# Attention block on one core: row maxima turned by one rounded product a query tile, diagonal tiles masked in PSUM by VectorE

## The chip, the cores and the metric

The kernel runs on one core of a Trainium2 chip. The metric is the device time of one execution in microseconds (us), lower is better.

## The reference

Two sequences of 2048 rows with 256 features pass through a layer norm, an attention of 16 heads with 64 features each, its output projection, a second norm, a small gated network and a third norm. What matters here is the attention:

```python
q = rope(hn @ Wq + bq); k = rope(hn @ Wk + bk); v = hn @ Wv + bv
attn = einsum('bihd,bjhd->bhij', q, k) * 64 ** -0.5
attn = where(tril, attn, -inf)
out = einsum('bhij,bjhd->bihd', softmax(attn), v) @ Wo + bo + h
```

Every softmax subtracts a row maximum before the exponential. Any number near the maximum does, as long as it is the same one for the whole row.

## The kernel before

**Pairs and groups.** Sixteen passes (`it` 0 to 15: eight pairs of heads for each of two sequences) run one behind the other. In a pass the two heads `a` of the pair lie on partitions 0 to 63 and 64 to 127. Queries are taken in four blocks of 512, keys in tiles of 128, so a pass has 40 score units (`UNITS`), two to a group, and 20 groups `g`. Every engine has its own list of work per group, written out by hand in `pair` of that engine, and the engines meet at counting semaphores.

**Work of PE (TensorE) in a group.** The order, in `pair` of the tensor block, is: first maxima unit, the group's two score units (L1221, L1223, L1225 and L1227, for diagonal units also the mask products L1231), second maxima unit, then in some groups the turning of the maxima (L1243, `turn_maxima`, in groups 1, 5, 11 and 19), or a piece of the next pass's projections (L1155 to L1157, groups 3, 4, 7, 8, 10, 13, 15, 17), a third maxima unit where there is one, the weighing of the values of the group before (L1261), and in groups 0, 2, 6 and 12 the sums of the exponentials (L1268).

**The maxima.** For the shift of the softmax the kernel computes the scores a second time, with the queries on partitions, coarsely. A maxima unit (t, c) is query tile t of 128 rows against key block c of up to 512 keys; `MUNITS` lists 40 of them a pass, and for each t the last one (c = t // 4) holds the diagonal. PE writes both heads' products into the single buffer `m_ps` (L1200). For a diagonal unit it then adds the causal mask on the last 128 keys by four small bf16 products (L1205: a mask of 64 rows times a 64 by 64 identity, two column halves for two heads). DVE (VectorE) takes the negated maximum over the keys from `m_ps` (L875) into `mpart`, and for the last unit of a tile reduces the parts into `mc` (L878). `mc` has one column for each block, tile and head. Maxima unit m + 1 may overwrite `m_ps` only when DVE has counted `maxed` for unit m; PE waits for that in `some_maxima`.

**The order on DVE in a group** (`pair` of the vector block): `turn_sums` (L915) of an ended block, `products` of the next pass's piece (L891, L895), the first two maxima, `piece_lo` (L909), `weights`, `invert` and `divide` (L920, L923, L928), `turned_sum` (L902, which waits for four DMAs that swap the halves of a head), and the third maximum.

**The turn.** The maxima must lie along the free axis of the score units. `turn_maxima` does this by eight fp32 products a block: for each of four tiles and each head, the column of `mc`, broadcast to 64 columns, is the stationary operand and the fp32 identity `id_f` the moving one; the result is 64 equal rows in each half of `x_ps`. ACT copies it, rounded to f32r, into `aux` (L599). In the scores, L1227 adds it by a product with `ones_r`, a matrix of 1/64, over the 64 equal rows of the head. An fp32 product shows as two MATMUL records in the trace, an f32r product as one.

```python
            def some_maxima(which):
                for m in which:
                    pe.wait_ge(maxed, it * NM + m)
                    maxima(it, par, m) ...
```

Of the kernel before, what the change touches and what calls it, by code (L numbers as in the profile page):

```python
# [5 lines left out]
ALU = mybir.AluOpType  # L6
ACT = mybir.ActivationFunctionType
AX = mybir.AxisListType
F32 = mybir.dt.float32
# [93 lines left out]
def postln_block_kernel(nc, h, gamma, beta, wqkv, bqk, bv, wo, bo, wgate_t, wup_t, wdown_t,  # L103
                        cos, sin, ident, masks, attn, hn_far, v_far, out):
    h, out = h.rearrange("b s d -> (b s) d"), out.rearrange("b s d -> (b s) d")
    with ExitStack() as ctx:
        def sb(name, shape, dt):
            return ctx.enter_context(nc.sbuf_tensor(name, shape, dt))
# [7 lines left out]
        cos_sb = sb("cos_sb", [P, SEQ], F32)  # L116
        sin_sb = sb("sin_sb", [P, SEQ], F32)
        id_f = sb("id_f", [P, P], F32)
        mask_b = sb("mask_b", [P, 4, P], BF16)
        id_b = sb("id_b", [P, DK], BF16)  # L120
        ones_r = sb("ones_r", [P, P], F32R)
        ones_f = sb("ones_f", [P, DK], F32)
        gam = sb("gam", [P, KC], F32)
        bet = sb("bet", [P, KC], F32)
# [1 line left out]
        w_raw = sb("w_raw", [P, KC, 2, P], F32)  # L126
        b_qk = sb("b_qk", [P, 2, 2], F32)
        b_v = sb("b_v", [P, OC], F32)
        mc = sb("mc", [P, BLOCKS, TG, 2], F32)
        mpart = sb("mpart", [P, 2, 2, BLOCKS], F32)  # L130
        r_i = sb("r_i", [P, NB // 32], F32)
        stats = sb("stats", [P, BATCH * TT, 6], F32)
# [128 lines left out]
        wv_hi = sem("wv_hi")  # L261
        wv_lo = sem("wv_lo")
        m_scored = sem("m_scored")
        maxed = sem("maxed")
        m_rows = sem("m_rows")
        m_turned = sem("m_turned")
        aux_done = sem("aux_done")
        scored = sem("scored")
# [64 lines left out]
        def _(sp):  # L333
# [124 lines left out]
            load_input(0, 3)  # L458
            load_b(0, 0)
            for dst, src in ((sin_sb[:, :], sin), (cos_sb[:, :], cos),  # L460
                             (mask_b[:, :, :], masks[:, 0:4 * P].rearrange("p (m n) -> p m n", m=4)),
                             (id_b[:, :], masks[:, 4 * P:4 * P + DK]), (b_v[:, :], bv),
                             (bo_sb[:, :], bo.partition_broadcast(P))):
                sp.dma_start(dst, src).then_inc(const_in, 16)
            for g in range(GROUPS):
# [109 lines left out]
        def _(act):  # L575
# [156 lines left out]
            affine(2)  # L732
            affine(3)
            root_input(3)
            for t in range(TG):
                evict_v_first(t)
            for i in range(4, TURNS):
# [83 lines left out]
        @block.vector  # L821
        def _(dve):
            nc.vector.memset(ones_f[:, :], 1.0).then_inc(o_stored, 16)
            nc.vector.memset(ones_r[:, :].bitcast(F32), 1.0 / DK).then_inc(out_stored, 16)
            nc.vector.memset(mc[:, :, :, :], 0.0).then_inc(normed, 1)
            nc.vector.memset(r_i[:, :], 0.0).then_inc(tile_done, 1)
            nc.vector.memset(pause[:, :], 0.0).then_inc(z_added, 1)
            nc.vector.memset(rstd[:, :], 0.0).then_inc(primed, 1)
# [35 lines left out]
            def weights(n):  # L864
                dve.wait_ge(w_hi, n + 1)
                nc.vector.tensor_tensor(w_hl[:, 1, :, :], w_raw[:, :, :, :].rearrange("p k j n -> p k (j n)"),
                                        w_hl[:, 0, :, :].bitcast(F32), ALU.subtract).then_inc(w_lo, 1)

            def maximum(n, m):

                t, c, w = MUNITS[m]
                dve.wait_ge(m_scored, n * NM + (m + 1))
                parts = t // TG + 1
                dst = mc[:, t // TG, t % TG, :] if parts == 1 else mpart[:, t % 2, :, c]
                nc.vector.tensor_reduce(dst, m_ps[:, :, 0:w], AX.X, ALU.max, negate=True).then_inc(maxed, 1)  # L875
                if parts > 1 and c == parts - 1:
                    dve.wait_ge(maxed, n * NM + (m + 1))
                    nc.vector.tensor_reduce(mc[:, t // TG, t % TG, :], mpart[:, t % 2, :, 0:parts],  # L878
                                            AX.X, ALU.min).then_inc(m_rows, 1)

            def rest_wv(n, raw):
# [271 lines left out]
        def _(pe):  # L1153
# [38 lines left out]
            def maxima(n, par, m):  # L1192

                t, c, w = MUNITS[m]
                if c == 0 and t % TG == 0:
                    pe.wait_ge(qk_hi, n * (2 * BLOCKS) + 2 * (t // TG + 1))
                diag = c == t // TG
                q, k = slice(t * P, (t + 1) * P), slice(NB * c, NB * c + w)
                for a, rows in enumerate(halves):
                    last = nc.tensor.matmul(m_ps[:, a, 0:w], qk[par][rows, 0, q], qk[par][rows, 1, k],  # L1200
                                            start=True, stop=not diag)
                if diag:
                    for x in range(2):
                        for a, rows in enumerate(halves):
                            last = nc.tensor.matmul(m_ps[:, a, w - P + DK * x:w - P + DK * (x + 1)],  # L1205
                                                    mask_b[rows, 2 + x, :], id_b[rows, :], start=False, stop=x == 1)
                last.then_inc(m_scored, 1)

            def scores(kind, it, par, u):
                blk, j, q0 = UNITS[u]  # L1210
                if kind is not FIRST or u >= 2:
                    pe.wait_ge(exped, it * NU + (u - 1))
                if j == 0:
                    pe.wait_ge(aux_done, it * BLOCKS + (blk + 1))
                    pe.wait_ge(qk_lo, it * (2 * BLOCKS) + 2 * (blk + 1))
                q, k = slice(NB * blk + q0, NB * (blk + 1)), slice(j * P, (j + 1) * P)
                two = 2 * (u % 2)
                dst = [s_ps[:, two + a, q0:NB] for a in range(2)]
                diag = j >= 4 * blk
                for a, rows in enumerate(halves):  # L1220
                    nc.tensor.matmul(dst[a], qk[par][rows, 1, k], qk[par][rows, 0, q], start=True, stop=False)  # L1221
                for a, rows in enumerate(halves):
                    nc.tensor.matmul(dst[a], qk[par][rows, 1, k], qk[par][rows, 2, q], start=False, stop=False)  # L1223
                for a, rows in enumerate(halves):
                    nc.tensor.matmul(dst[a], qk[par][rows, 3, k], qk[par][rows, 0, q], start=False, stop=False)  # L1225
                for a, rows in enumerate(halves):
                    last = nc.tensor.matmul(dst[a], ones_r[rows, :], aux[rows, q0:NB], start=False, stop=not diag)  # L1227
                if diag:
                    for x in range(2):
                        for a, rows in enumerate(halves):  # L1230
                            last = nc.tensor.matmul(s_ps[:, two + a, q0 + DK * x:q0 + DK * (x + 1)],  # L1231
                                                    mask_b[rows, x, :], id_b[rows, :], start=False, stop=x == 1)
                last.then_inc(scored, 1)

            def turn_maxima(n, blk):

                if blk == 0:
                    pe.wait_ge(maxed, n * NM + TG)
                else:
                    pe.wait_ge(m_rows, n * (TT - TG) + TG * blk)  # L1240
                for t in range(TG):
                    for a, rows in enumerate(halves):
                        last = nc.tensor.matmul(x_ps[rows, t * P:(t + 1) * P], mc[:, blk, t, a:a + 1].broadcast_to([P, DK]),  # L1243
                                                id_f[:, :], start=True, stop=True, skip_group_check=True)
                last.then_inc(m_turned, 1)

            def weigh(kind, it, par, g):
# [143 lines left out]
            for m in range(TG, 2 * TG):  # L1391
                first_maximum(m)
                project_v_first(2 * TG + m)
            pe.wait_ge(v_done, TT - 1)
            turn_maxima(0, 0)
            for m in range(2 * TG, PROLOGUE_MAXIMA):
                first_maximum(m)
# [140 lines left out]
```

## Time and profile before

| what | value |
|---|---|
| time, median of 3 runs | 2189.78 us (2185.9 to 2190.99) |
| the profiled execution: its time | 2190.48 us |
| its span in the trace | 2188.7 us |
| PE busy | 2073.8 us, 95% |
| DVE busy | 1549.2 us, 71% |
| ACT / POOL busy | 915.9 us / 1401.2 us |
| mean granted TensorE clock | 0.986 of full speed |

Busy time counts the union of the intervals of an engine's instructions. PE's matmuls are pipelined and overlap in the records, so a record's length (0.40 us for 512 columns) is not what the matmul takes from the stream: that is the distance from one start to the next. "PEld" is the loading of the stationary operand, which can run beside an earlier matmul.

### The profile page before, as it was taken

Reading aid. Unit: us, or ns where it says so; the run is one execution under the profiler, and the core shown is the slowest. Engines: PE = TensorE matmul, PEld = TensorE weight load, DVE = VectorE, ACT = ScalarE, POOL = GpSimd, SP = SyncE. Lnnn points to the kernel's source line nnn. Section 1 sums busy time; section 2 is a strip of 40 time slices with the busy share of each in tenths; the row PEclk is TensorE's granted clock in tenths of the full one; section 3 lists DMA queues with packets and bytes.
Section 4 is the critical chain, followed back from the end, with each engine's and each line's share of the span. In section 5 each row is a group of like instructions: output and inputs, shape, how many; then the busy total and the mean of one; then the engine's idle time right before and its main releaser. Section 6 shows DMA issues by size and latency. Waiting matters only on the chain.

```text
span 2188.7 us, 38909 instructions
## 1 busy us (share of the span) xinstructions
PE 2073.8 (95%) x15488; PEld 1311.4 (60%) x15488; DVE 1549.2 (71%) x2181; ACT 915.9 (42%) x1262; POOL 1401.2 (64%) x1206
## 2 busy tenths in 40 slices
PE   6889999999999999999999999999999989999997
PEld 5555555555555555555555555555555545788986
DVE  7577767676778776767767777767777765666654
ACT  4434343444343434434344444443444344534442
POOL 3368777777787876677878787878787878100000
PEclk9899999999999999999999999999999999999999
DMA  6411212121212122122121212121112131222200
GB/s 207 132 44 46 57 42 61 38 65 35 61 32 63 33 74 69 46 67 68 44 59 44 59 44 59 44 59 34 49 35 55 34 131 44 76 93 75 98 10 29
DMA packets 116154, 132.25 MB, mean 60 GB/s; under 512 B 15248, under 2 KB 71184, under 8 KB 115728
## 3 DMA queue, kind: packets, MB, share of 16 engines
q1 hardware_dynamic: 115984, 129.92, 20.1%
q8 instruction: 115, 1.88, 0.4%
q14 instruction: 55, 0.45, 0.1%
HBM read 56.47 MB, written 39.85 MB: 44 GB/s over the span
## 4 chain that ended last, share of the span: by engine, by line
PE 68%; DVE 20%; DMA 3%; issue 3%; SPq 3%; ACT 2%; POOL 1%; ACTq 0%; DVEq 0%
PE o_ps L1261 15%; DVE mpart L875 8%; PE m_ps L1200 8%; PE s_ps L1221 5%; PE s_ps L1225 4%; PE s_ps L1227 4%; PE s_ps L1223 4%; PE x_ps L1155 3%; DMA rot<-qr 3%; SPq L387 3%; DVE qc L902 3%; PE x_ps L1243 3%; PE x_ps L1268 2%; PE x_ps L1157 2%; PE x_ps L1156 2%
## 5 line engine op out<-in xcount | busy, mean ns | idle before, releaser
L561 POOL TENSOR_TENSOR acc<-acc,pt 128x512 f32<-128x512 f32 (+3 forms) x1024 | 1199.1, 1204 | 209.5 <-ACT pt L615 209.1
L875 DVE TENSOR_REDUCE mpart<-m_ps 128x2 f32<-128x1024 f32 (+2 forms) x576 | 625.0, 1085 | 309.6 <-PE m_ps L1200 227.4
L615 ACT ACTIVATE pt<-s_ps 128x1024 f32<-128x1024 f32 (+3 forms) x640 | 544.3, 896 | 701.4 <-PE s_ps L1227 334.3
L1261 PE MATMUL o_ps<-pt,v 128*64 128x512 f32 (+3 forms) x2560 | 538.1, 541 | 0.0
L1200 PE MATMUL m_ps<-qk 64*128 64x512 f32 (+3 forms) x1280 | 288.1, 446 | 62.6 <-DVE mpart L875 52.9
L1200 PEld LDWEIGHTS m_ps<-qk 64*128 64x128 f32 x1280 | 120.7, 185 | 367.9 <-DVE mpart L875 211.4
L1261 PEld LDWEIGHTS o_ps<-pt,v 128*64 128x64 f32 x2560 | 159.7, 137 | 222.6 <-issue 202.6
L556 POOL TENSOR_TENSOR acc<-pt 128x512 f32<-128x512 f32 (+1 forms) x128 | 166.8, 1325 | 160.5 <-ACT pt L615 160.5
L1221 PE MATMUL s_ps<-qk 64*128 64x512 f32 (+3 forms) x1280 | 253.4, 392 | 0.0
L1225 PE MATMUL s_ps<-qk 64*128 64x512 f32 (+3 forms) x1280 | 234.7, 362 | 0.0
L1227 PE MATMUL s_ps<-aux,ones_r 64*128 64x512 f32 (+3 forms) x1280 | 234.7, 362 | 0.0
L1223 PE MATMUL s_ps<-qk 64*128 64x512 f32 (+3 forms) x1280 | 234.1, 362 | 0.0
L902 DVE TENSOR_TENSOR qc<-qc,rot 128x512 f32<-128x512 f32 x128 | 141.2, 1105 | 101.7 <-DMA rot<-qr 101.5
L593 ACT ACTIVATE qk<-qc 128x512 fp32r<-128x512 f32 x128 | 80.2, 629 | 221.0 <-DVE qc L902 221.0
L909 DVE TENSOR_TENSOR qk<-qc,qk 128x512 fp32r<-128x512 f32 x120 | 139.0, 1158 | 0.0
L1225 PEld LDWEIGHTS s_ps<-qk 64*128 64x128 f32 x1280 | 121.2, 185 | 19.7
L1227 PEld LDWEIGHTS s_ps<-aux,ones_r 64*128 64x128 f32 x1280 | 121.2, 185 | 19.0
L1223 PEld LDWEIGHTS s_ps<-qk 64*128 64x128 f32 x1280 | 121.9, 186 | 17.2
L1221 PEld LDWEIGHTS s_ps<-qk 64*128 64x128 f32 x1280 | 121.9, 187 | 15.6 <-ACT pt L615 4.1
L1155 PE MATMUL x_ps<-hn,w_hl 128*128 128x512 f32 x240 | 108.4, 452 | 0.0
L1156 PE MATMUL x_ps<-hn,w_hl 128*128 128x512 f32 x240 | 95.4, 397 | 0.0
L1157 PE MATMUL x_ps<-hn,w_hl 128*128 128x512 f32 x240 | 95.2, 397 | 0.0
(168 smaller groups left out, 2883.1 us busy)
## 6 DMA issues: line engine op xcount, KB each, us to landing
rot<-qr SPq DMA_DIRECT2D x512, 64.0 KB, 2.0
attn<-o_sum SPq DMA_DIRECT2D x64, 256.0 KB, 2.3
o_raw<-attn SPq DMA_DIRECT2D x8, 2048.0 KB, 9.0
v<-v_far SPq DMA_DIRECT2D x16, 768.0 KB, 5.3
v_far<-v_part SPq DMA_DIRECT2D x48, 256.0 KB, 2.0
w_raw<-in_wqkv SPq DMA_DIRECT2D x34, 128.0 KB, 4.8
v_far<-v SPq DMA_DIRECT2D x16, 256.0 KB, 2.6
v<-v_far SPq DMA_DIRECT2D x16, 256.0 KB, 4.5
```

What stands on the lines that cost most here:

```text
L556: last = nc.gpsimd.tensor_tensor(sums, pt[:, (u - 1) % SLOTS, a, q0:NB], probs, ALU.add)
L561: nc.gpsimd.tensor_tensor(sums, sums, probs, ALU.add).then_inc(summed, 1)
L615: nc.scalar.activation(pt[:, u % SLOTS, :, q0:NB], s_ps[:, two:two + 2, q0:NB], ACT.Exp, scale=SCALE)\
L875: nc.vector.tensor_reduce(dst, m_ps[:, :, 0:w], AX.X, ALU.max, negate=True).then_inc(maxed, 1)
L902: nc.vector.tensor_tensor(qc[:, c % 2, a, :], qc[:, c % 2, a, :], rot[:, a, :], ALU.add).then_inc(roped, 1)
L1155: nc.tensor.matmul(dst, lhs[0], rhs[0], start=first, stop=False)
L1200: last = nc.tensor.matmul(m_ps[:, a, 0:w], qk[par][rows, 0, q], qk[par][rows, 1, k], start=True, stop=not diag)
L1221: nc.tensor.matmul(dst[a], qk[par][rows, 1, k], qk[par][rows, 0, q], start=True, stop=False)
L1223: nc.tensor.matmul(dst[a], qk[par][rows, 1, k], qk[par][rows, 2, q], start=False, stop=False)
L1225: nc.tensor.matmul(dst[a], qk[par][rows, 3, k], qk[par][rows, 0, q], start=False, stop=False)
L1227: last = nc.tensor.matmul(dst[a], ones_r[rows, :], aux[rows, q0:NB], start=False, stop=not diag)
L1261: last = nc.tensor.matmul(o_ps[rows, q0:NB], v[par][:, j, rows], pt[:, u % SLOTS, a, q0:NB], start=(j == 0), stop=(j == n - 1), skip_group ...
```

## The change

It has two edits and what they need.

1. The turn: `mc` becomes f32r, DVE rounds when it writes the maxima, and has 132 columns a block. The maxima of tile t of a block go to columns t (head 0) and 64 + t (head 1). The slice of 128 columns that begins at t is the stationary operand of one f32r product with a rounded identity `id_r`; row 0 of the result holds the maxima of head 0, row 64 those of head 1, other rows hold values that nobody uses. `ones_r` becomes `pick_r`, zero but for ones in rows 0 and 64, so that L1227's product, of unchanged size, picks the row. There are four products a block in place of eight.
2. The mask of the maxima: PE's four mask products a diagonal unit go. DVE adds a bf16 mask of 128 by 128 to the last 128 keys of both heads in `m_ps`, waits until the result has landed, and then takes the maximum.

The mask products of the score units (L1231) stay.

```diff
-        mask_b = sb("mask_b", [P, 4, P], BF16)
+        id_r = sb("id_r", [P, P], F32R)
+        mask_b = sb("mask_b", [P, 3, P], BF16)
-        ones_r = sb("ones_r", [P, P], F32R)
+        pick_r = sb("pick_r", [P, P], F32R)
-        mc = sb("mc", [P, BLOCKS, TG, 2], F32)
+        mc = sb("mc", [P, BLOCKS, P + TG], F32R)
...
             root_input(3)
+            nc.scalar.activation(id_r[:, :], id_f[:, :], ACT.Copy).then_inc(id_rounded, 1)
...
-            nc.vector.memset(ones_r[:, :].bitcast(F32), 1.0 / DK).then_inc(out_stored, 16)
-            nc.vector.memset(mc[:, :, :, :], 0.0).then_inc(normed, 1)
+            nc.vector.memset(pick_r[:, :].bitcast(F32), 0.0).then_inc(out_stored, 15)
+            dve.wait_ge(out_stored, 15)
+            for a in range(2):
+                last = nc.vector.memset(pick_r[DK * a:DK * a + 1, :].bitcast(F32), 1.0)
+            last.then_inc(out_stored, 1)
+            nc.vector.memset(mc[:, :, :].bitcast(F32), 0.0).then_inc(normed, 1)
...
+            def row_maxima(t):
+                return mc[:, t // TG, 0:P].rearrange("p (a i) -> p a i", a=2)[:, :, t % TG]
+
             def maximum(n, m):
 
                 t, c, w = MUNITS[m]
                 dve.wait_ge(m_scored, n * NM + (m + 1))
                 parts = t // TG + 1
-                dst = mc[:, t // TG, t % TG, :] if parts == 1 else mpart[:, t % 2, :, c]
+                dst = row_maxima(t) if parts == 1 else mpart[:, t % 2, :, c]
+                if c == parts - 1:
+
+                    own = m_ps[:, :, w - P:w]
+                    nc.vector.tensor_tensor(own, own, mask_b[:, 2, :].unsqueeze(1).broadcast_to([P, 2, P]),
+                                            ALU.add).then_inc(m_masked, 1)
+                    dve.wait_ge(m_masked, n * TT + (t + 1))
                 nc.vector.tensor_reduce(dst, m_ps[:, :, 0:w], AX.X, ALU.max, negate=True).then_inc(maxed, 1)
                 if parts > 1 and c == parts - 1:
                     dve.wait_ge(maxed, n * NM + (m + 1))
-                    nc.vector.tensor_reduce(mc[:, t // TG, t % TG, :], mpart[:, t % 2, :, 0:parts],
+                    nc.vector.tensor_reduce(row_maxima(t), mpart[:, t % 2, :, 0:parts],
                                             AX.X, ALU.min).then_inc(m_rows, 1)
...
-                diag = c == t // TG
...
                     last = nc.tensor.matmul(m_ps[:, a, 0:w], qk[par][rows, 0, q], qk[par][rows, 1, k],
-                                            start=True, stop=not diag)
-                if diag:
-                    for x in range(2):
-                        for a, rows in enumerate(halves):
-                            last = nc.tensor.matmul(m_ps[:, a, w - P + DK * x:w - P + DK * (x + 1)],
-                                                    mask_b[rows, 2 + x, :], id_b[rows, :], start=False, stop=x == 1)
+                                            start=True, stop=True)
...
-                    last = nc.tensor.matmul(dst[a], ones_r[rows, :], aux[rows, q0:NB], start=False, stop=not diag)
+                    last = nc.tensor.matmul(dst[a], pick_r[rows, :], aux[rows, q0:NB], start=False, stop=not diag)
...
                 for t in range(TG):
-                    for a, rows in enumerate(halves):
-                        last = nc.tensor.matmul(x_ps[rows, t * P:(t + 1) * P], mc[:, blk, t, a:a + 1].broadcast_to([P, DK]),
-                                                id_f[:, :], start=True, stop=True, skip_group_check=True)
+                    last = nc.tensor.matmul(x_ps[:, t * P:(t + 1) * P], mc[:, blk, t:t + P],
+                                            id_r[:, :], start=True, stop=True, skip_group_check=True)
...
             pe.wait_ge(v_done, TT - 1)
+            pe.wait_ge(id_rounded, 1)
             turn_maxima(0, 0)
```

## Rows read from the trace of the kernel before

**Rows 1.** The page: busy time and share of the span, then the chain by engine.
```profile
PE 2073.8 (95%) x15488; PEld 1311.4 (60%) x15488; DVE 1549.2 (71%) x2181; ACT 915.9 (42%) x1262; POOL 1401.2 (64%) x1206
PE 68%; DVE 20%; DMA 3%; issue 3%; SPq 3%; ACT 2%; POOL 1%; ACTq 0%; DVEq 0%
```

**Rows 2.** Timeline of PE in pass 8: start us, length us, then the instruction.
```profile
1006.70 0.27 PE L1227 MATMUL s_ps<-aux,ones_r 64*128 64x128 f32 x2
1006.81 0.23 PE L1231 MATMUL s_ps<-id_b,mask_b 64*128 64x64 bf16 x4
1006.98 1.09 PE L1243 MATMUL x_ps<-id_f,mc 128*64 128x128 f32 x16
1007.90 1.67 PE L1261 MATMUL o_ps<-pt,v 128*64 128x512 f32 x8
...
1053.84 0.39 PE L1156 MATMUL x_ps<-wv_hl,hn 128*128 128x512 f32 x1
1054.07 0.39 PE L1157 MATMUL x_ps<-wv_hl,hn 128*128 128x512 f32 x1
1054.39 1.94 PE L1261 MATMUL o_ps<-pt,v 128*64 128x512 f32 x8
```

**Rows 3.** Groups of instructions, 1868 to 1871 us: busy us, mean ns, idle before.
```profile
L1410 PE MATMUL gu_ps<-id_f,x_g 128*128 128x128 f32 x8 | 1.1, 280 | 2.1 <-DVE x_g L1043 2.1
```

**Rows 4.** Waits, whole span: us in total, times, longest us.
```profile
PEld o_ps L1261 <- ACT pt L615: 7.8, 30, 0.3
DVE qc L902 <- DMA rot<-qr: 101.5, 78, 3.9
```

**Rows 5.** Timeline of PE, diagonal unit (11, 2), then the next maxima unit.
```profile
1124.63 0.50 PE L1200 MATMUL m_ps<-qk 64*128 64x512 f32 x2
1124.97 0.24 PE L1205 MATMUL m_ps<-id_b,mask_b 64*128 64x64 bf16 x4
1125.04 0.48 PE L1221 MATMUL s_ps<-qk 64*128 64x512 f32 x2
1125.35 0.40 PE L1223 MATMUL s_ps<-qk 64*128 64x512 f32 x2
1125.58 0.40 PE L1225 MATMUL s_ps<-qk 64*128 64x512 f32 x2
...
1126.97 0.40 PE L1200 MATMUL m_ps<-qk 64*128 64x512 f32 x2
```

**Rows 6.** Groups of instructions on DVE by shape, whole span.
```profile
L891 DVE SCALAR_TENSOR_TENSOR qr<-x_ps,b_qk,sin_sb 128x512 f32<-128x512 f32 x120 | 88.8, 740 | 2.3 <-PE x_ps L1157 2.3
L1113 DVE SCALAR_TENSOR_TENSOR out_g<-z_ps,x_keep 128x512 f32<-128x512 f32 x2 | 1.4, 688 | 4.3 <-PE z_ps L1157 4.3
L875 DVE TENSOR_REDUCE mpart<-m_ps 128x2 f32<-128x512 f32 x48 | 32.6, 679 | 31.5 <-PE m_ps L1205 31.5
L875 DVE TENSOR_REDUCE mpart<-m_ps 128x2 f32<-128x256 f32 x48 | 20.3, 422 | 20.1 <-PE m_ps L1205 20.1
L883 DVE TENSOR_TENSOR wv_hl<-wv_raw,wv_hl 128x512 fp32r<-128x512 f32 x6 | 8.1, 1347 | 1.5 <-ACT wv_hl L624 1.5
```

**Rows 7.** Timeline of DVE in pass 9: units (11, 2), (4, 1), (5, 0) and (13, 3).
```profile
1125.39 1.19 DVE L875 TENSOR_REDUCE mpart<-m_ps 128x2 f32<-128x1024 f32 x1
1126.61 0.16 DVE L878 TENSOR_REDUCE mc<-mpart 128x2 f32<-128x6 f32 x1
...
1076.52 0.41 DVE L875 TENSOR_REDUCE mpart<-m_ps 128x2 f32<-128x256 f32 x1
...
1078.35 1.22 DVE L875 TENSOR_REDUCE mpart<-m_ps 128x2 f32<-128x1024 f32 x1
...
1147.97 0.65 DVE L875 TENSOR_REDUCE mpart<-m_ps 128x2 f32<-128x512 f32 x1
```

**Rows 8.** Timeline of PE in pass 9: the maxima units behind (5, 0) and (13, 3).
```profile
1079.62 0.39 PE L1200 MATMUL m_ps<-qk 64*128 64x256 f32 x2
...
1148.67 0.50 PE L1200 MATMUL m_ps<-qk 64*128 64x512 f32 x2
```

More of the change, by code:

```diff
@@ L263, in postln_block_kernel @@
         m_scored = sem("m_scored")
+        m_masked = sem("m_masked")
         maxed = sem("maxed")
         m_rows = sem("m_rows")
+        id_rounded = sem("id_rounded")
         m_turned = sem("m_turned")
@@ L460, in _ @@
             for dst, src in ((sin_sb[:, :], sin), (cos_sb[:, :], cos),
-                             (mask_b[:, :, :], masks[:, 0:4 * P].rearrange("p (m n) -> p m n", m=4)),
-                             (id_b[:, :], masks[:, 4 * P:4 * P + DK]), (b_v[:, :], bv),
+                             (mask_b[:, :, :], masks[:, 0:3 * P].rearrange("p (m n) -> p m n", m=3)),
+                             (id_b[:, :], masks[:, 3 * P:3 * P + DK]), (b_v[:, :], bv),
                              (bo_sb[:, :], bo.partition_broadcast(P))):
@@ L1508 @@
     r, k = np.arange(P)[:, None] % DK, np.arange(P)[None, :]
-    masks = [np.where(later, np.float32(MASKED), np.float32(0))
-             for later in (k > r, k > r + DK, r > k, r + DK > k)]
+    row = np.arange(P)[:, None]
+    masks = [np.where(later, np.float32(MASKED), np.float32(0)) for later in (k > r, k > r + DK, k > row)]
     def with_first(a, n):
```

## The prediction

> **What bounds the kernel now.** I read the page first, then PE's timeline over two groups of a pass, then DVE's timeline beside it. The page shows PE busy for 95% and DVE for 71%, and a chain that is PE for 68% and DVE for 20% [rows 1]. So a microsecond off PE's stream is worth something in most places, but in a fifth of the span DVE is what everything waits for, and the change takes from PE and gives to DVE. The question is at which of the sixteen diagonal units of a pass PE has time to spare and at which it waits for `maxed`. That is read unit by unit from the two timelines, as the distance between the end of DVE's reduction and the next L1200.
>
> Three patterns are seen. In the first the next L1200 comes 0.5 to 0.6 us behind the end of the reduction (tiles 1, 2 and 6) or over 2 us behind (tiles 0, 5, 8, 9, 10, 12 and 15), as a weighing of up to 1.9 us lies between [rows 2]. In the second DVE ends little before: unit (11, 2) ends at 1125.39 + 1.19 = 1126.58 and the next L1200 starts at 1126.97 [rows 5, 7]. In the third PE is held: the reduction of (13, 3) ends at 1147.97 + 0.65 = 1148.62, and L1200 starts at 1148.67 [rows 7, 8].
>
> **Edit 1, the turn.** The sixteen records of L1243 take from 1006.98 to 1007.90, 0.92 us of PE's stream [rows 2], once in each of 64 blocks. The new turn is four products of 128 columns with a full array of weights. Nothing of that form is in the attention, but the eight transposes of the same form L1410 take 1.1 us in all with a last record of 0.28, so (1.1 - 0.28) / 7 = 0.12 us each [rows 3], and a pair of score products of 128 columns takes 1006.81 - 1006.70 = 0.11 [rows 2]. I take 0.11. The last one is followed by a weighing in another tiling of the array; at such a change, from L1157 to L1261, 0.32 us pass where 0.23 pass between like products (1053.84 to 1054.07) [rows 2]. A 512-column stream accounts for 0.23 - 0.02 = 0.21, so 0.11 are the change of tiling, and behind a stream of a quarter the length, 0.05, the step is 0.16 us. The new turn: 3 x 0.11 + 0.16 = 0.49 us, a saving of 0.43. What comes in front (1006.81 to 1006.98) stays. Bounds: 3 x 0.05 + 0.16 = 0.31 us if only the stream counted (saving 0.61), and 4 x 0.28 = 1.12 us if nothing overlapped (a loss of 0.20); I stay at the transposes and the score pairs, the nearest rows.
>
> Is it paid? The turn is always followed by the weighing, which hardly waits for ACT (7.8 us in 30 waits over the whole span) [rows 4], so the stream moves up at once. In groups 1, 11 and 19 the maxima units behind it have over 2 us in hand. In group 5 they do not: DVE is then in a sequence of `products`, swap by DMA and `turned_sum` (101.5 us of DVE's waits are for that DMA [rows 4]) that began before the turn, and the unit after the next is held by it. There I count nothing. So three turns a pass: 48 x 0.43 = **21 us off**.
>
> Against this stands a rule of the Trainium skill, page "TensorE: Matmul & The Clock Gate", section on packing small matmuls: a weight load runs beside an earlier matmul only if the two use different row groups, which the new full-array products do not. By it each product would pay its load and its stream, by the page's formula for loads an estimated 107 + 53 = 160 ns, and edit 1 would save some 10 us less. The transposes at 0.12 us use the same row groups and speak against it.
>
> **Edit 2 on PE.** At unit (11, 2) the four mask products hold the stream from 1124.97 to 1125.04, 0.07 us, and the first score product behind them takes 0.31 (1125.04 to 1125.35) where the next takes 0.23, so 0.08 more: together 0.15 us [rows 5]. I take 0.15 us for every diagonal unit, sixteen a pass. It is paid where PE is not held afterwards: nine of the first pattern, 9 x 16 x 0.15 = **22 us off**. For tile 12 (unit (12, 3)), I count nothing, as with the turn of group 5 that follows it.
>
> **Edit 2 on DVE.** The added add reads two heads of 128 columns from PSUM with a bf16 operand from SBUF and writes PSUM. Nothing in the trace writes PSUM from DVE. The nearest rows are operations on PSUM with an SBUF operand: 740 ns and 688 ns for 512 columns [rows 6]. The reduction shows the slope, 679 ns for 512 and 422 for 256, so 257 ns less for half: 0.43 to 0.48 us; I take 0.44, as the mask is small and L891 runs evenly beside POOL's work. The reduction must wait until the result has landed. DVE's dependent step L878 starts 1126.61 - 1126.58 = 0.03 us after its source ended [rows 7]. So a maximum becomes **0.47 us** later, and 256 of them add 120 us to DVE's busy 1549. Bounds: 0.26 us if only the columns counted (the slope alone), and 0.74 + 0.03 if a write to PSUM doubled the work.
>
> Who waits for it: the reduction stands behind the add, everything later in DVE's list behind both, and PE's next maxima unit behind the count.
> - Pattern 1: hidden. Where the gap is near 0.55 (tiles 1, 2, and the unit (6, 1)), 0.55 - 0.05 covers 0.47 barely.
> - Pattern 2: L1200 starts 0.39 after DVE ended; a held one starts 0.05 after, but with 0.11 of weight load inside its record (0.50 against 0.40 long [rows 5, 8]). The cover is 0.39 - 0.05 - 0.11 = 0.23, the delay 0.47 - 0.23 = 0.24. There are three a pass, tiles 3, 7 and 11: 0.72 us.
> - Pattern 3: the whole 0.47, at tiles 13 and 14; and at tile 4, because its reduction at 1076.52, L891, L895 and the next reduction, that ends at 1078.35 + 1.22 = 1079.57, stand without a gap, and PE starts at 1079.62 [rows 7, 8]. Three a pass: 1.41 us.
> - Tile 12's add lies in DVE's wait for the swap of halves, and costs nothing; if that wait were gone it would cost another 0.47.
>
> Sum: 2.13 us x 16 = **34 us on**. In some passes DVE is further behind than in the two that I read unit by unit, where it splits weights (L883, six times, 1347 ns [rows 6]) or the next sequence's input (eight times): some ten stretches in which a saving is lost and an add paid, about 0.5 us each, **5 us on**.
>
> **The rest.** ACT's rounding of the identity, two short memsets and a larger one of `mc` lie ahead of the first loads' landing or beside PE's prologue; the mask DMA is smaller. L1227 keeps its shape. Each at nothing; if the cover were gone, under 1 us in all. The eight diagonal units of the prologue are inside the sixteen passes counted.
>
> **Sum.** 21 + 22 - 34 - 5 = 4 us off. Against the profiled execution's own 2190.5 us that is 2186.5; that execution lay 0.7 above the median of the three, so **2186 us**.
>
> **The rivals.**
> 1. *DVE becomes the bound (slower).* Place: the adds at tiles 13, 14, 4, and 3, 7, 11. Each 0.1 us more for the add costs 6 x 16 x 0.1 = 9.6 us, so from 0.51 us for add and wait on nothing is gained, and from 0.56 the kernel is slower by over 0.2%. With the upper bound 0.77 the six cost 29 us more and the three of 0.5 cover begin to delay PE by 0.3 each, 14 more: 2229. For it: no row of DVE writing PSUM, and the order on DVE, where L902 behind it also runs beside POOL. Against: 740 ns hardly vary. Chance 0.28.
> 2. *The adds hide better than I count.* If the delays of pattern 2 are taken up by the groups behind and the fourth turn is paid, 12 + 7 less: 2167. For it: DVE idles for 29% of the span. Chance 0.14.
> 3. *The new products do not overlap their weight loads*, and a turn takes 4 x 0.05 us more: 48 x 0.2 = 10 us, 2196. This is the rule cited above. Chance 0.05.
> 4. *The turn does not do what it says*, because ACT's copy or a wait behind it holds the stream anyway: 21 us back, 2207. Against it stands the 7.8 us of waits. Chance 0.05.
>
> **How the numbers follow.** My forecast has 0.48, with its own range of 2178 to 2195. About 0.2%, 4.4 us, is what a measurement of this kernel can tell from no change. The forecast lies on that edge: of its 0.48 I give 0.26 to faster, 0.17 to no change, 0.05 to slower. Rival 1 gives 0.24 to slower and 0.04 to no change, rival 2 all to faster, rival 3 half to either, rival 4 all to slower. Faster 0.40, same 0.24, slower 0.36. The range takes in most of rival 2 and rival 1 up to an add of 0.65: 2168 to 2208.
>
> **What would show it.** Right: L1243's four products within 0.5 us of the stream; no L1205; the first score product behind a diagonal unit at 0.23; the add at 0.42 to 0.48 us; DVE busy near 1665 us; idle of L1200 behind DVE up, at tiles 3, 4, 7, 11, 13 and 14 alone. Wrong: an add over 0.55 us, L1200 held behind tiles 1, 2 or 6, `turned_sum` or `products` late behind the adds with PE waiting for `x_ps`, or turns of 0.7 us.

## The result, and the profile of the changed kernel

The changed kernel takes 2240.45 us (median of 4 runs, 2237.5 to 2246.3) against 2190.39: a ratio of 1.0234, 95% interval 1.0222 to 1.0247. It is 50 us slower, outside the range that was given, and on the side of rival 1. The ground that rival 1 was priced by did not come, though: the add takes what was forecast.

The page of the changed kernel, busy times and chain by engine, which answer to [rows 1], then the costliest maxima group of PE:

```profile
PE 2064.5 (92%) x13696; PEld 1271.7 (57%) x13696; DVE 1674.2 (75%) x2439; ACT 918.0 (41%) x1263; POOL 1405.8 (63%) x1206
PE 50%; DVE 33%; DMA 5%; issue 5%; SPq 5%; ACT 2%; POOL 1%; ACTq 0%; DVEq 0%
L1216 PE MATMUL m_ps<-qk 64*128 64x512 f32 (+3 forms) x1280 | 296.5, 460 | 127.6 <-DVE mpart L892 94.5
```

PE lost 9 us of busy time and 1792 records, as it should. DVE gained 125 us, near the 120 forecast. The chain went from 68% PE and 20% DVE to 50% and 33%, and DMA with its issue (SPq), which is mostly the swap of halves, from 6% to 10%: PE sets the pace in half of the span where it did in two thirds.

Groups of DVE, busy us, mean ns, idle before. In the kernel before:

```profile
L902 DVE TENSOR_TENSOR qc<-qc,rot 128x512 f32<-128x512 f32 x128 | 141.2, 1105 | 101.7 <-DMA rot<-qr 101.5
L909 DVE TENSOR_TENSOR qk<-qc,qk 128x512 fp32r<-128x512 f32 x120 | 139.0, 1158 | 0.0
L928 DVE TENSOR_TENSOR o_sum<-o_sum,r_t 128x512 f32<-128x512 f32 x64 | 56.7, 887 | 2.2
```

and in the changed one:

```profile
L919 DVE TENSOR_TENSOR qc<-qc,rot 128x512 f32<-128x512 f32 x128 | 136.3, 1067 | 82.0 <-DMA rot<-qr 81.9
L889 DVE TENSOR_TENSOR m_ps<-m_ps,mask_b 128x256 f32<-128x256 f32 x256 | 107.8, 421 | 91.3 <-PE m_ps L1216 91.0
L926 DVE TENSOR_TENSOR qk<-qc,qk 128x512 fp32r<-128x512 f32 x120 | 146.6, 1222 | 0.0
L945 DVE TENSOR_TENSOR o_sum<-o_sum,r_t 128x512 f32<-128x512 f32 x64 | 68.9, 1076 | 2.2
```

The add (L889) takes 421 ns; 0.44 us was assumed. The nearest operation that reads PSUM and SBUF and writes SBUF, L1084 in the same trace, takes 684 ns for 512 columns; less the 257 ns of the slope that is an estimated 427 ns for 256, so no extra price of writing PSUM is to be seen. What was not forecast are the other rows, three operations with both operands in SBUF and the same work as before. `piece_lo` (L909 before, L926 now) and the division (L928, L945) have become longer, 139.0 to 146.6 us and 56.7 to 68.9 us; `turned_sum` (L902, L919) has become shorter, 141.2 to 136.3 us.

**Where the time went.** The distances between the starts of consecutive maxima units on PE, averaged over passes 1 to 15 of both traces, add up to a pass. The largest differences, in us a pass (a minus is faster):

| from unit to unit | before | changed | difference |
|---|---|---|---|
| (0, 0) to (1, 0), holds a turn | 4.25 | 3.88 | -0.37 |
| (9, 2) to (10, 0), holds a turn | 4.09 | 3.66 | -0.43 |
| (10, 2) to (11, 0), holds a turn | 4.15 | 3.72 | -0.43 |
| (13, 0) to (13, 1), holds a turn | 4.39 | 4.03 | -0.35 |
| (1, 0) to (2, 0) | 2.24 | 2.60 | +0.36 |
| (3, 0) to (4, 0) | 2.34 | 3.51 | +1.17 |
| (7, 0) to (7, 1) to (8, 0) | 4.81 | 5.83 | +1.03 |
| (12, 1) to (12, 2) | 3.03 | 3.81 | +0.78 |
| (13, 3) to (14, 0) | 2.38 | 2.83 | +0.45 |
| all forty | | | +3.3 |

3.3 us in sixteen passes are 53 us: the whole loss. It sits in a handful of places, and the turn is a gain wherever PE runs freely.

The largest place, tile 3, on DVE's timeline. Before:

```profile
1066.59 0.69 DVE L902 TENSOR_TENSOR qc<-qc,rot 128x512 f32<-128x512 f32 x1 [2.86 <-DMA rot<-qr]
1067.20 0.68 DVE L875 TENSOR_REDUCE mc<-m_ps 128x2 f32<-128x512 f32 x1
1069.17 0.96 DVE L875 TENSOR_REDUCE mc<-m_ps 128x2 f32<-128x768 f32 x1 [1.28 <-PE m_ps L1205]
1070.04 0.68 DVE L909 TENSOR_TENSOR qk<-qc,qk 128x512 fp32r<-128x512 f32 x1
1070.83 0.72 DVE L915 STREAM_TRANSPOSE r_t<-x_ps 128x512 f32<-128x512 f32 x1
1071.47 1.19 DVE L875 TENSOR_REDUCE mc<-m_ps 128x2 f32<-128x1024 f32 x1
```

Changed:

```profile
1096.36 0.69 DVE L919 TENSOR_TENSOR qc<-qc,rot 128x512 f32<-128x512 f32 x1 [3.50 <-DMA rot<-qr]
1096.97 0.43 DVE L889 TENSOR_TENSOR m_ps<-m_ps,mask_b 128x256 f32<-128x256 f32 x1
1097.43 0.69 DVE L892 TENSOR_REDUCE mc<-m_ps 128x2 fp32r<-128x512 f32 x1
1098.66 0.43 DVE L889 TENSOR_TENSOR m_ps<-m_ps,mask_b 128x256 f32<-128x256 f32 x1 [0.54 <-PE m_ps L1216]
1099.13 0.96 DVE L892 TENSOR_REDUCE mc<-m_ps 128x2 fp32r<-128x768 f32 x1
1100.01 1.45 DVE L926 TENSOR_TENSOR qk<-qc,qk 128x512 fp32r<-128x512 f32 x1
1101.37 0.70 DVE L932 STREAM_TRANSPOSE r_t<-x_ps 128x512 f32<-128x512 f32 x1
1102.00 0.40 DVE L889 TENSOR_TENSOR m_ps<-m_ps,mask_b 128x256 f32<-128x256 f32 x1
1102.43 1.23 DVE L892 TENSOR_REDUCE mc<-m_ps 128x2 fp32r<-128x1024 f32 x1
```

Two things are to be seen. First, the stretch begins with `turned_sum` at the landing of a DMA. PE's unit (1, 0) had long been there (1094.73), so what PE saved ahead of it became a longer wait: from (0, 0) to (2, 0) the changed kernel is 0.01 us a pass faster than the one before, where the kernel without any mask of the maxima (`turn_no_mask`, below) is 0.43 faster. Second, L926 takes 1.45 us where it took 0.68. POOL's timeline over the same place, changed kernel:

```profile
1099.62 2.99 POOL L559 TENSOR_TENSOR acc<-pt 128x512 f32<-128x512 f32 x2 [4.59 <-ACT pt L618]
```

and before:

```profile
1070.10 3.03 POOL L556 TENSOR_TENSOR acc<-pt 128x512 f32<-128x512 f32 x2 [3.58 <-ACT pt L615]
```

Before, DVE's instruction began 0.06 us ahead of POOL's two additions and ran at its own speed; it was POOL's first addition that took 1.77 us, and its second 1.30. Now DVE's begins at 1100.01, 0.39 us behind POOL's start. By the two records behind POOL's merged row its first addition takes 1.28 and ends at 1100.90, and its second takes 1.75; DVE's instruction ends 0.55 us behind that first addition, at 1101.45. By the Trainium skill, page "SBUF — State Buffer", section "SBUF: two separate sides", an instruction of DVE with two SBUF inputs and one of GpSimd that reads SBUF exclude each other, and whoever starts first keeps the shared ports to its end. These rows agree: each waits for the other's end. The adds, with one operand in PSUM, take 0.39 to 0.43 us in all 256 places and never grow, which agrees too. The prediction did not use the rule.

### The profile page after: what moved, and what is told of

Its sections match the earlier page's. It is cut to its first block, busy times and chain, and to the rows that moved or that the text cites. A ratio compares the mean times of both kernels' runs of the same rounds, so it can differ in the third digit from the quotient of the medians.

```text
span 2244.5 us, 35584 instructions
## 1 busy us (share of the span) xinstructions
PE 2064.5 (92%) x13696; PEld 1271.7 (57%) x13696; DVE 1674.2 (75%) x2439; ACT 918.0 (41%) x1263; POOL 1405.8 (63%) x1206
## 4 chain that ended last, share of the span: by engine, by line
PE 50%; DVE 33%; DMA 5%; issue 5%; SPq 5%; ACT 2%; POOL 1%; ACTq 0%; DVEq 0%
DVE mpart L892 11%; PE o_ps L1271 11%; PE m_ps L1216 7%; DMA rot<-qr 5%; SPq L390 5%; DVE qk L926 4%; DVE qc L919 3%; DVE qr L908 3%; PE s_ps L1232 3%; PE s_ps L1236 2%; PE s_ps L1238 2%; PE s_ps L1234 2%; DVE m_ps L889 2%; PE x_ps L1172 2%; PE gu_ps L1172 2%
## 5 line engine op out<-in xcount | busy, mean ns | idle before, releaser
L1271 PE MATMUL o_ps<-pt,v 128*64 128x512 f32 (+3 forms) x2560 | 544.7, 547 | 0.0
L1216 PE MATMUL m_ps<-qk 64*128 64x512 f32 (+3 forms) x1280 | 296.5, 460 | 127.6 <-DVE mpart L892 94.5
L1271 PEld LDWEIGHTS o_ps<-pt,v 128*64 128x64 f32 x2560 | 156.9, 137 | 234.2 <-issue 201.6
L1238 PE MATMUL s_ps<-aux,pick_r 64*128 64x512 f32 (+3 forms) x1280 | 237.4, 366 | 0.0
L919 DVE TENSOR_TENSOR qc<-qc,rot 128x512 f32<-128x512 f32 x128 | 136.3, 1067 | 82.0 <-DMA rot<-qr 81.9
L889 DVE TENSOR_TENSOR m_ps<-m_ps,mask_b 128x256 f32<-128x256 f32 x256 | 107.8, 421 | 91.3 <-PE m_ps L1216 91.0
L926 DVE TENSOR_TENSOR qk<-qc,qk 128x512 fp32r<-128x512 f32 x120 | 146.6, 1222 | 0.0
L1238 PEld LDWEIGHTS s_ps<-aux,pick_r 64*128 64x128 f32 x1280 | 122.3, 187 | 19.6
L1172 PE MATMUL x_ps<-hn,w_hl 128*128 128x512 f32 x240 | 108.2, 451 | 0.0
L1173 PE MATMUL x_ps<-hn,w_hl 128*128 128x512 f32 x240 | 95.4, 397 | 0.0
```

Of the source, the lines that this page charges most:

```text
L919: nc.vector.tensor_tensor(qc[:, c % 2, a, :], qc[:, c % 2, a, :], rot[:, a, :], ALU.add).then_inc(roped, 1)
L926: nc.vector.tensor_tensor(qk[par][:, 2 + a, here], qc[:, c % 2, a, :], qk[par][:, a, here].bitcast(F32), ALU.subtract).then_inc(qk_lo, 1)
L1172: nc.tensor.matmul(dst, lhs[0], rhs[0], start=first, stop=False)
L1238: last = nc.tensor.matmul(dst[a], pick_r[rows, :], aux[rows, q0:NB], start=False, stop=not diag)
L1271: last = nc.tensor.matmul(o_ps[rows, q0:NB], v[par][:, j, rows], pt[:, u % SLOTS, a, q0:NB], start=(j == 0), stop=(j == n - 1), skip_group ...
```

## The experiments

### One edit at a time, and PE's side without DVE's

`turn_alone` has edit 1 with the masks of the maxima left to PE:

```diff
+DVE_MASKED = ()
...
-                if c == parts - 1:
+                if c == parts - 1 and t in DVE_MASKED:
 
                     own = m_ps[:, :, w - P:w]
...
+                on_pe = c == t // TG and (True)
+                if on_pe:
+                    for x in range(2):
+                        for a, rows in enumerate(halves):
+                            last = nc.tensor.matmul(m_ps[:, a, w - P + DK * x:w - P + DK * (x + 1)],
+                                                    mask_b[rows, 3 + x, :], id_b[rows, :], start=False, stop=x == 1)
```

> Edit 1 alone; the masks of the maxima stay on PE. Theory A (in the changed kernel the adds stand one behind another in DVE's list, in stretches that no PE event starts, and nearly all of them are paid; the turn itself is a gain): the turn takes 0.5 us less of PE's stream in each of 64 blocks or a little less, part of it swallowed by waits for maxed, so 12 to 22 us below the kernel before. Theory B (the new turn or what hangs on it is at fault: full-array products, the copy, the picking product): at or above the kernel before, up to +50 us.

Measured: 2182.75 us, ratio 0.9953 (0.9936 to 0.9970). Edit 1 is a gain of 7 us by the medians (the interval allows 7 to 14), so Theory B falls; the gain is at the lower end of what Theory A gave or under it.

`mask_alone` is the kernel before with edit 2 alone (`turn_maxima`, `mc` and `ones_r` as before; L1205 out, DVE's add in).

> Edit 2 alone: the turn is the one of before by fp32 products, DVE adds the mask. Theory A: the whole loss and more, 60 to 75 us above the kernel before. Theory B: under 20 us above it.

Measured: 2246.36 us, ratio 1.0255 (1.0223 to 1.0286), 56 us above. The whole loss is edit 2's. It is a little under the range of Theory A and far from Theory B.

`turn_no_mask` takes the add out and puts nothing in, so its maxima run over later keys of the diagonal tile too:

```diff
+DVE_MASKED = ()
...
-                if c == parts - 1:
+                if c == parts - 1 and t in DVE_MASKED:
```

> The changed kernel without any mask of the maxima: neither PE's products nor DVE's add, so the row maxima are taken over later keys of the diagonal tile too (the scores of the softmax keep their mask). It shows what PE's side of both edits is worth without DVE's. Theory A: 30 to 45 us below the kernel before, 80 to 95 us below the changed one. Theory C (DVE was the bound all along and PE's savings are worth little): under 20 us below the kernel before, by the turn alone or less.

Measured: 2155.13 us, ratio 0.9826 (0.9792 to 0.9860), 28 us below `turn_alone` and 85 below the changed kernel. PE's half of edit 2 is worth 28 us, if DVE gets nothing in return. Both figures lie in Theory A's ranges, and Theory C falls.

`turn_both_masks` puts PE's products back and keeps the add (of the diff of `turn_alone`, the part from `on_pe` on alone).

> The changed kernel with PE's mask products put back beside DVE's add, so the mask is added twice. Against turn_alone it is the price of 256 adds and their waits on DVE and nothing else. Theory A: 5 to 15 us above the changed kernel and 70 to 85 us above turn_alone, that is 0.3 us for each add of 0.45. Theory C (the removal of the mask products was worth nothing): the same time as the changed kernel.

Measured: 2234.59 us, ratio 1.0193 (1.0162 to 1.0224). The 256 adds cost 2234.59 - 2182.75 = 52 us, 0.20 us each, under the 70 to 85 of Theory A. The surprise is the other comparison: with PE's 1024 mask products put back the kernel is 6 us faster than the changed one, not 5 to 15 slower. What saved 28 us without the adds saves nothing beside them, as Theory C had it. One place shows why that can be. DVE's timeline around the division ahead of unit (12, 1), changed kernel:

```profile
1160.36 0.71 DVE L940 STREAM_TRANSPOSE r_t<-r_i 128x512 f32<-128x512 f32 x1
1161.11 1.78 DVE L945 TENSOR_TENSOR o_sum<-o_sum,r_t 128x512 f32<-128x512 f32 x1
1162.81 1.21 DVE L892 TENSOR_REDUCE mpart<-m_ps 128x2 f32<-128x1024 f32 x1
```

and `turn_both_masks`:

```profile
1155.91 0.71 DVE L940 STREAM_TRANSPOSE r_t<-r_i 128x512 f32<-128x512 f32 x1
1156.66 0.71 DVE L945 TENSOR_TENSOR o_sum<-o_sum,r_t 128x512 f32<-128x512 f32 x1
1157.29 1.21 DVE L892 TENSOR_REDUCE mpart<-m_ps 128x2 f32<-128x1024 f32 x1
```

The same division takes 1.78 us in one and 0.71 in the other; in the mean over passes 1.72 and 0.71 (0.94 in the kernel before), and the step from (12, 1) to (12, 2) is 1.01 us a pass longer, 16 us in all. A saving of some tenths on PE moved the division into POOL's work. That accounts for 16 of the 34 us between a gain of 28 and a loss of 6; for the rest no single place was found.

### How much of the adds' price is POOL?

Both kernels have POOL's sums of the exponentials cut from up to 512 columns to 16, with a memset of `acc` ahead of the passes. They leave out most of the softmax's denominators:

```diff
-                        sums = acc[:, blk % 2, a, q0:NB]
-                        probs = pt[:, u % SLOTS, a, q0:NB]
+                        sums = acc[:, blk % 2, a, q0:q0 + 16]
+                        probs = pt[:, u % SLOTS, a, q0:q0 + 16]
```

> turn_alone with POOL's sums of the exponentials cut to 16 columns (the denominators are left out but for those), so that POOL hardly works beside DVE. DVE's instructions with two operands in SBUF (L902, L909, L928 of the kernel before) are to fall from 0.9 to 1.1 us in the mean to 0.7. Either theory: 15 to 50 us below turn_alone. It is the base for light_both_masks.

Measured: 2120.01 us, ratio 0.9677 (0.9658 to 0.9695), 63 us below `turn_alone` and more than expected. At most that much of the kernel's time hangs on DVE instructions that stand behind POOL's; whatever else waits for POOL gets shorter in this kernel too.

> turn_both_masks with POOL's sums cut to 16 columns (the denominators are left out but for those). Against light_turn_alone it is the price of the 256 adds without POOL beside DVE. Theory A1 (a shifted DVE falls into POOL's work, and that is a good part of the 52 us that the adds cost with POOL): 15 to 35 us above light_turn_alone. Theory A2 (the adds cost by their own length in series with PE's waits, POOL has no part): 45 to 60 us above it.

Measured: 2150.92 us, ratio 0.9823 (0.9805 to 0.9841). The adds now cost 2150.92 - 2120.01 = 31 us, against 52 with POOL at work. Groups of DVE in `light_both_masks`:

```profile
L922 DVE TENSOR_TENSOR qc<-qc,rot 128x512 f32<-128x512 f32 x128 | 89.1, 698 | 82.0 <-DMA rot<-qr 81.6
L929 DVE TENSOR_TENSOR qk<-qc,qk 128x512 fp32r<-128x512 f32 x120 | 82.4, 687 | 0.0
L948 DVE TENSOR_TENSOR o_sum<-o_sum,r_t 128x512 f32<-128x512 f32 x64 | 44.3, 692 | 2.2
```

All three stand at 0.69 to 0.70 us now. And at tile 3, on its timeline:

```profile
1044.67 0.68 DVE L929 TENSOR_TENSOR qk<-qc,qk 128x512 fp32r<-128x512 f32 x1
1045.27 0.71 DVE L935 STREAM_TRANSPOSE r_t<-x_ps 128x512 f32<-128x512 f32 x1
1045.90 0.40 DVE L892 TENSOR_TENSOR m_ps<-m_ps,mask_b 128x256 f32<-128x256 f32 x1
1046.34 1.23 DVE L895 TENSOR_REDUCE mc<-m_ps 128x2 fp32r<-128x1024 f32 x1
```

The measured 31 us lie in Theory A1's range and far from A2's: some 21 of the 52 us go with POOL's load. But they are not all instructions that the adds pushed behind POOL. Busy time of the three groups in each kernel, in us:

| | `turned_sum` | `piece_lo` | division | sum |
|---|---|---|---|---|
| `turn_alone` | 142.2 | 139.4 | 56.7 | 338.3 |
| `turn_both_masks` | 137.7 | 145.1 | 58.4 | 341.2 |
| `light_turn_alone` | 89.3 | 82.6 | 44.3 | 216.2 |
| `light_both_masks` | 89.1 | 82.4 | 44.3 | 215.8 |

With POOL at work the adds lengthen the three groups by 3 us in all: some instances grow and others shrink. What counts is where. At tile 3 `piece_lo` grows from 0.68 to 1.40 us, and the adds lengthen the step from (3, 0) to (4, 0) by 1.12 us a pass with POOL at work (`turn_both_masks` against `turn_alone`) and by 0.40 without. These 0.72 us are 12 of the 21 us. Other places point at a second reason: the step behind (13, 3) costs 0.43 us a pass with POOL and nothing without, and in the kernel without POOL's load DVE's list is 122 us shorter, so that DVE has time to spare there (in `turn_alone` PE starts 0.06 us behind the reduction of (13, 3), in `light_turn_alone` 0.71). This pair cuts POOL everywhere, so it does not part new collisions from the slack that the old ones had used up.

### Which adds are paid?

`adds_1_2_3` and `hybrid5` leave the mask to PE except for the named tiles (`t in DVE_MASKED` on DVE, `t not in DVE_MASKED` on PE).

> Edit 1, and DVE's add in place of PE's mask products for query tiles 1, 2 and 3 alone. The prediction counted 0.24 us a pass for them (tile 3) less 0.3 saved on PE, so about the time of turn_alone. Theory A (the three adds stand in one stretch of DVE's list that begins with turned_sum, so at the landing of a DMA and not at an event of PE; all are paid, and the piece_lo behind them falls into POOL's work and takes twice as long): 1.0 to 1.4 us a pass, 16 to 22 us above turn_alone, a third of the whole price for three of sixteen adds.

Measured: 2197.21 us, ratio 1.0032 (1.0021 to 1.0043), 14.5 us above `turn_alone`, a little under Theory A's range: 0.30 us for each of 48 adds, PE's savings already taken off. The places in its trace and in that of `turn_alone`, us behind unit (0, 0) on PE, means over passes 1 to 15:

| | `turn_alone` | `adds_1_2_3` |
|---|---|---|
| PE starts (2, 0) | 6.31 | 6.26 |
| PE starts (3, 0) | 8.34 | 8.28 |
| DVE starts `piece_lo` behind tile 2 | 7.67 | 8.07 |
| POOL starts its two additions | 7.85 | 7.71 |
| length of that `piece_lo` | 0.68 | 1.46 |
| PE starts (4, 0) | 10.69 | 11.80 |

The adds of tiles 1 and 2 are hidden from PE's units (2, 0) and (3, 0). But tile 2's leaves DVE's list behind it 0.40 us later, which puts `piece_lo` behind POOL's start instead of ahead of it, where it takes 0.78 us more; with the add of tile 3 all of it stands in front of the reduction that unit (4, 0) waits for.

> Edit 1, and DVE's add in place of PE's mask products for query tiles 5, 8, 9, 12 and 15 alone, the ones behind which the changed kernel shows PE's next maxima unit still 0.4 us or more behind DVE. Theory A (the price is set by the place of an add, not by its number): these five are hidden and PE's savings of 0.08 to 0.15 us each are kept, 3 to 9 us below turn_alone. Rival (each add costs 0.2 us wherever it stands, as DVE's share of the span is what counts): 5 x 16 x 0.2 less 8 = 8 us above it.

Measured: 2171.29 us, ratio 0.9911 (0.9889 to 0.9934), 11.5 us below `turn_alone`, a little more than Theory A gave, and 19 below the kernel before. Five adds a pass in the right places cost nothing that can be seen, and PE keeps 0.08 us at four of them and 0.15 at (9, 2), 7.5 us in all. The rest may be chance of timing: `piece_lo` takes 129.1 us in sum here and 139.4 in `turn_alone`. The rival of an equal price falls.

`hybrid5_twice` makes each of these five adds twice, with a wait each.

> hybrid5 with the add of its five tiles made twice, each time with its wait, so 80 adds of 0.45 us more in DVE's list and nothing else changed. Theory A (these places have 0.4 us and more behind the first add): 0 to 6 us above hybrid5, under 0.08 us an add. Rival (0.2 us an add wherever it stands): 16 us above it.

Measured: 2174.40 us (2164.3 to 2180.2), ratio 0.9930 (0.9903 to 0.9957). It lies 3 us above `hybrid5` and within its own spread. By the medians 80 adds more cost 0.04 us each there; at the average of 0.20 us it would have been 16, which is above the slowest of the four runs.

`hybrid7` hands tiles 0 and 10 to DVE as well.

> hybrid5 with tiles 0 and 10 handed to DVE as well. Tile 0's add lies in DVE's wait for the swapped halves, tile 10's ends ahead of PE's next but one. Theory A: PE saves 0.10 and 0.15 us a pass, the adds cost 0 to 0.15: from 4 us below hybrid5 to 2 above it. Rival (0.2 us for every add): 3 us above it and more.

Measured: 2171.12 us, ratio 0.9906 (0.9880 to 0.9932), the same as `hybrid5`. At tile 0 PE gains 0.10 us a pass and loses 0.06 of it at the next unit.

### A move that failed

`late_lo` puts `piece_lo` behind the group's other work in the changed kernel:

```diff
-                    if g - 2 in PIECE and kind is not LAST:
-                        piece_lo(it + 1, *PIECE[g - 2], 1 - par)
...
                     for m in ms[2:]:
                         maximum(it, m) if m < NM else maximum(it + 1, m - NM)
+                    if g - 2 in PIECE and kind is not LAST:
+                        piece_lo(it + 1, *PIECE[g - 2], 1 - par)
```

> The changed kernel with one step of DVE moved within its group: piece_lo, with both operands in SBUF, stands behind the third maximum and the division instead of ahead of them. The work is the same. Theory A1 (behind the adds piece_lo falls into POOL's work just where PE's next maximum waits for what is behind it, tile 3 above all): 8 to 20 us below the changed kernel, and the step from unit (3, 0) to (4, 0) shorter by 0.7 us or more. Theory A2 (the length of the adds alone): within 5 us of the changed kernel.

Measured: 2252.63 us, ratio 1.0275 (1.0248 to 1.0303), 12 us slower than the changed kernel. Neither theory's range holds it. It was ill chosen for the place it was meant for: group 12 has no third maximum and no `products`, so `piece_lo` still stands ahead of tile 3, whose step did not change (+0.03 us). Elsewhere the move did harm, above all behind (7, 1), +0.75 us a pass. It says nothing against or for the collision at tile 3.

> The same move in hybrid5, whose tiles 1 to 3 are masked by PE. Theory A1: little to gain, as piece_lo behind tile 2 takes 0.68 us there already: between 10 us below hybrid5 and 3 above it. A gain as large as that of late_lo over the changed kernel would say that the move is worth something whether the adds are there or not.

Measured: 2191.12 us, ratio 0.9995 (0.9981 to 1.0009), 20 us slower than `hybrid5`, outside the expectation. The move costs with and without the adds, and not by collisions: the three groups with two SBUF operands take 312 us in sum here and 325 in `hybrid5`, and 336 in `late_lo` against 352 in the changed kernel. What it costs by is the order. Behind (7, 0) in `hybrid5_late_lo`:

```profile
973.17 1.23 DVE L893 TENSOR_REDUCE mpart<-m_ps 128x2 f32<-128x1024 f32 x1 [0.87 <-PE m_ps L1218]
974.31 1.03 DVE L927 TENSOR_TENSOR qk<-qc,qk 128x512 fp32r<-128x512 f32 x1
975.26 0.74 DVE L909 SCALAR_TENSOR_TENSOR qr<-x_ps,b_qk,sin_sb 128x512 f32<-128x512 f32 x1
975.92 0.73 DVE L913 SCALAR_TENSOR_TENSOR qc<-x_ps,b_qk,cos_sb 128x512 f32<-128x512 f32 x1
976.58 1.21 DVE L893 TENSOR_REDUCE mpart<-m_ps 128x2 f32<-128x1024 f32 x1
```

`piece_lo` (L927) now stands between two reductions that PE waits for, with the products behind it; in `hybrid5` it stood ahead of the first, at 964.38, and ran while DVE had to wait for PE. The second reduction came 2.46 us behind the first there and comes 3.41 behind it here.

## Why the prediction was wrong

**The turn** was mis-sized. The four products and the way out of them, changed kernel, timeline of PE:

```profile
1092.32 0.23 PE L1242 MATMUL s_ps<-id_b,mask_b 64*128 64x64 bf16 x4
1092.48 0.66 PE L1253 MATMUL x_ps<-id_r,mc 128*128 128x128 f32 x4
1093.08 1.72 PE L1271 MATMUL o_ps<-pt,v 128*64 128x512 f32 x8
1094.73 0.39 PE L1216 MATMUL m_ps<-qk 64*128 64x256 f32 x2
```

They hold the stream for 1093.08 - 1092.48 = 0.60 us, where 0.49 was forecast and 0.92 stood before [rows 2]. The distances of their starts in the trace are 0.17, 0.11 and 0.11, and 0.20 to the weighing: the step of 0.11 between like products was right, and the first and the last cost 0.05 more each than forecast. The weighing behind takes 0.05 more as well, and in `turn_alone` the three free turns of a pass save 0.27 to 0.28 each, not 0.43: 13 us. The fourth, of group 5, for which nothing was counted, shortens its step by 0.41, of which the next loses 0.10. Other steps, above all the one behind (14, 3) with 0.24, become longer, and 7 us are left by the medians. By the rule of the Trainium skill that the prediction cites (page "TensorE: Matmul & The Clock Gate", section on packing small matmuls: full-array loads do not overlap a matmul) each product would take an estimated 0.16. The trace does not agree: the four weight loads start 0.11 us apart. That the sum comes near 4 x 0.16 = 0.64 is by the first and the last step.

**PE's mask products** were worth 0.15 us only behind (1, 0), (9, 2) and (10, 2); behind the other unhindered tiles, in `turn_no_mask` against `turn_alone`, 0.07 to 0.11. The 22 us were too many for the nine tiles; without the adds all sixteen give 28.

**The add itself** was right: 421 ns, and 0.03 to the reduction. Rival 1 was priced by an add of 0.56 us and more, and that did not come. It named in passing that L902 behind the adds also runs beside POOL; that ground was right in kind, and it had neither a place nor a price.

**The step that failed is "Pattern 1: hidden", with "delay 0.47 - 0.23" of pattern 2.** I measured the cover of each add from the end of its own reduction to PE's next L1200, and let its effect end there. For tiles 1 and 2 that cover was right in `adds_1_2_3`: PE's next units come no later. But the 0.40 us that tile 2's add sets DVE's list back stay in the list and come out at the next unit that waits for DVE, here (4, 0). In the changed kernel the stretch also starts later against PE (`turned_sum` 4.53 us behind unit (0, 0), 4.42 in `turn_alone`), and tile 1's add is paid too. It was an error to judge the adds one by one: three adds in one stretch cost 14.5 us net, where the sum had 4 us for tile 3 and a saving of 5 for tiles 1 and 2. Without POOL's load all 256 adds cost 31 us. 34 were forecast in this term, which is close in size, but in part by other places: without POOL's load tile 4's add shows as forecast (0.40 us a pass behind unit (5, 0)) and tile 3's costs 0.40 for 0.24, while tiles 13 and 14 cost nothing for 0.94, and 0.28 and 0.15 come behind (15, 0) and (1, 0), where none was counted.

**What was left out altogether is the collision with POOL.** L902, L909 and L928 with two SBUF operands take 0.69 us alone and up to 1.8 behind POOL. The prediction used L891 to say that the add does not collide, which was right, and put the instructions behind the add at their old lengths without a reason. Two places show what that was worth in the changed kernel: the `piece_lo` ahead of tile 3, 0.68 to 1.45 us, and the division ahead of unit (12, 1), 0.94 to 1.72. Both lengthen a step that PE waits in, by 0.77 and 0.78 us a pass, together 25 of the 53 us that the steps lose. Which instruction meets POOL is in part luck: with PE's mask products put back the division is clear of POOL again, and the kernel 6 us faster. The sum came to 4 us off; the changed kernel came 50 on.

A version that beats both kernels is `hybrid5` at 2171 us. `turn_no_mask` is faster still, 2155 us, and shifts the softmax by a maximum that may include later keys of the same tile; it stands only as long as such a key is not so far above the row's own that the exponentials vanish, which no run here explored for other inputs.

## What to carry to other kernels

When work is moved to an engine that has 29% of idle time, look for what starts each of its stretches. An added instruction that is hidden from the very next waiter still sets back the list behind it, and can be paid by a later one. Then list which instructions behind the added ones share something with a third engine: here a shift of 0.4 us doubled one. Moving the work only at the places with 0.4 us and more behind them made the kernel 11 us faster than leaving all of it on PE; moving all of it made it 58 us slower.

## What the runs showed of the hardware

- A DVE instruction on PSUM with one SBUF operand that writes PSUM in place takes 0.42 us for 256 elements and stays there beside POOL (`after`, L889). DVE instructions with two SBUF operands of 512 elements take 0.69 to 0.70 us with POOL nearly idle (`light_both_masks`) and 1.07 to 1.22 us in the mean with it (`after`). With POOL's sums cut, `turn_alone` is 63 us shorter.
- Four f32r products of 128 columns with full-array weights start 0.11 us apart. The step from the first to the second, behind a change of tiling, is 0.17, and from the last to a product of another tiling 0.20 (`after`, L1253 and L1271).
